# Two-sequence pre-norm transformer layer on 8 cores: the quantized GELU chain regrouped into three VectorE phases with one wait per step

## Chip, cores, metric

One Trainium2 chip, 8 cores. Every core runs the same program on two of the 16 sequences; the cores do not talk to each other. The metric is the device time of one execution in microseconds, that of the slowest core. Engines: TensorE (PE in the rows; PEld are its weight loads), VectorE (DVE), ScalarE (ACT), GpSimd (POOL) and SyncE (SP), the last two issuing DMAs here.

## The reference

```python
# x: (16, 2048, 1024) fp32
x = x + attn(layernorm(x))          # 16 heads of 64, w_qkv 1024x3072, w_proj 1024x1024
h = float2fix(layernorm(x) @ w1 + b1)      # w1 1024x4096; round to multiples of 1/256
xq = float2fix(h)
y = interp(xq, 33 points of exact GELU on [-4, 4]); y = where(xq > 4, xq, where(xq < -4, 0, y))
h = float2fix(float2fix(y))
x = x + float2fix(h @ w2 + b2)             # w2 4096x1024
```

`float2fix` rounds to multiples of 2^-8. The GELU is piecewise linear between the 33 points, so the kernel quantizes, finds the segment and the fraction, takes GELU at both ends of the segment, and interpolates.

## The kernel before

The program is a list of events in the order of emission, one list per engine; each engine runs its own in order, and counting semaphores join them: `c_pe` for PE, `c_v` for DVE, `c_s` for ACT. A wait is always on a count.

Stage A (0 to some 2200 us) is the first layer norm, QKV, attention and the output projection. The change does not touch it. Its layer norm shows (L204, L206, L216) an operation of DVE followed by a drain and a no-op that carries the increment, and ACT waiting for it.

Stage B is the feed-forward part: 8 blocks (`bi`) of 512 tokens, in each 32 column groups of 128 (`hm`), together 256 steps `g` or `h`. The main loop runs over `g`. In step `g` it emits, in this order:

- the w2 matmuls of the block before, `w2_mm` (L1073, 32 matmuls, 8 such groups to a block, at `hm` 3, 6, ..., 24), and their output eviction `w2_ev` on DVE (L1097, L1102, L1104, at `hm` 5, 8, ..., 26);
- the DMAs of w1 on GpSimd (L798);
- `act_E012(g)`: 8 W1 matmuls into one of two halves of `pA` (L935), free again when the eviction of `g-2` is done; the eviction on ACT (L950, times 256 plus bias, into `ft`); on DVE clamp and round (L961, drain, L964);
- pieces of the layer norm for the next block, in `hm` 3 to 20: loads; statistics on DVE (L841 to L846) and the square root on ACT (L855, with a table load ahead of it and one behind it, for the next GELU); reciprocal on DVE (L866, L868) and the apply on ACT (L880); transposes on PE (L894) and the copy of them on DVE (L905);
- `act_E34(g-1)`: ACT scales into `fu5` (L977); DVE rounds, subtracts, adds 0.5 (L985, L987, L990, with drains between);
- `act_E56(g-2)`: ACT computes two GELUs (L1006, L1008); DVE takes the difference and combines (L1017, L1019, L1022, with drains between);
- `act_E78(g-3)`: ACT adds a large constant and rescales into `gbuf` (L1039, drain, L1041).

Before L950, L977, L1006 and L1039 ACT has a `drain` as well, behind the wait. Every DVE group waits for the ACT instruction that feeds it and for nothing later, except that L961 also waits for the GELUs of `h-3`. The w2 matmuls of a block wait until its last `gbuf` is written (`g_done_of`); that happens in step `hm` 2 of the next block. All buffers are rings: `ft` and `fki` of four, `fu5` of three, `fji`, `fgl` of two.

Of the kernel before, what the change touches and what calls it, by code (L numbers as in the profile page):

```python
# [10 lines left out]
ALU = mybir.AluOpType  # L11
# [38 lines left out]
def build():  # L50
# [15 lines left out]
    p = Prog()  # L66
    with es:
# [844 lines left out]

        e1_hist = {}
        e5_hist = {}
        e6_hist = {}
        e8_hist = {}

        def act_E012(h):
            bi, hm = divmod(h, 32)
            hb = hm % 2  # L920
            i = h % 3
            i4 = h % 4
            grp = hm // 2
            sl = grp % 2

            def ev(t, bi=bi, hm=hm, hb=hb, sl=sl,
                   xd=xn2_ready[bi], wl=(w1load[(bi, grp)] if hm % 2 == 0 else None),
                   ag=e1_hist.get(h - 2)):
                t.wait_ge(c_v.sem, xd)
                if wl is not None:  # L930
                    t.wait_ge(c_lw[sl].sem, wl)
                if ag is not None:
                    t.wait_ge(c_s.sem, ag)
                for dc in range(NDC):
                    ins = t.matmul(pA[:, hb * 512:(hb + 1) * 512],  # L935
                                   w1s[:, sl, dc, (hm % 2) * 128:(hm % 2 + 1) * 128],
                                   xn2[:, bi % 2, dc, :],
                                   start=(dc == 0), stop=(dc == NDC - 1))
                ins.then_inc(c_pe.sem, 1)
            p.on("tensor", ev)  # L940
            c_pe.n += 1
            w1mm[(bi, grp)] = c_pe.n
            w1_pe = c_pe.n

            def ev(sc, hm=hm, hb=hb, i4=i4, w=w1_pe, vg=e6_hist.get(h - 4)):
                sc.wait_ge(c_pe.sem, w)
                if vg is not None:
                    sc.wait_ge(c_v.sem, vg)
                sc.drain()
                sc.activation(ft[:, i4, :], pA[:, hb * 512:(hb + 1) * 512], AF.Identity,  # L950
                              bias=b256[:, hm:hm + 1], scale=256.0).then_inc(c_s.sem, 1)
            p.on("scalar", ev)
            c_s.n += 1
            e1_hist[h] = c_s.n
            sid_done = c_s.n

            def ev(v, i=i, i4=i4, w=sid_done, sg=e5_hist.get(h - 3)):
                v.wait_ge(c_s.sem, w)
                if sg is not None:
                    v.wait_ge(c_s.sem, sg)  # L960
                v.tensor_scalar(fki[:, i4, :], ft[:, i4, :], -1152.5, 1152.5,  # L961
                                ALU.max, ALU.min)
                v.drain()  # L963
                v.tensor_scalar(ft[:, i4, :], fki[:, i4, :], MC, -MC,  # L964
                                ALU.add, ALU.add).then_inc(c_v.sem, 1)
            p.on("vector", ev)
            c_v.n += 1
            e1_hist[(h, "va")] = c_v.n

        def act_E34(h):  # L970
            i = h % 3
            i4 = h % 4

            def ev(sc, i=i, i4=i4, w=e1_hist[(h, "va")]):
                sc.wait_ge(c_v.sem, w)
                sc.drain()  # L976
                sc.activation(fu5[:, i, :], ft[:, i4, :], AF.Identity,  # L977
                              bias=p155[:, 0:1], scale=1.0 / 64.0).then_inc(c_s.sem, 1)
            p.on("scalar", ev)
            c_s.n += 1  # L980
            u5_done = c_s.n

            def ev(v, i=i, i4=i4, w=u5_done):
                v.wait_ge(c_s.sem, w)
                v.tensor_scalar(fki[:, i4, :], fu5[:, i, :], MC, -MC, ALU.add, ALU.add)  # L985
                v.drain()  # L986
                v.scalar_tensor_tensor(ft[:, i4, :], fki[:, i4, :], -1.0, fu5[:, i, :],  # L987
                                       ALU.mult, ALU.add)
                v.drain()
                v.tensor_scalar(fu5[:, i, :], ft[:, i4, :], 0.5, None,  # L990
                                ALU.add).then_inc(c_v.sem, 1)
            p.on("vector", ev)
            c_v.n += 1
            e1_hist[(h, "vb")] = c_v.n

        def act_E56(h):
            i = h % 3
            i4 = h % 4
            j = h % 2

            def ev(sc, i=i, j=j, w=e1_hist[(h, "vb")], fg=e6_hist.get(h - 2)):
                sc.wait_ge(c_v.sem, w)
                if fg is not None:
                    sc.wait_ge(c_v.sem, fg)
                sc.drain()
                sc.activation(fgl[:, j, :], fki[:, i4, :], AF.Gelu, bias=neg4[:, 0:1],  # L1006
                              scale=0.25)
                sc.activation(fji[:, j, :], fki[:, i4, :], AF.Gelu, bias=neg375[:, 0:1],  # L1008
                              scale=0.25).then_inc(c_s.sem, 1)
            p.on("scalar", ev)  # L1010
            c_s.n += 1
            e5_hist[h] = c_s.n
            s3_done = c_s.n

            def ev(v, i=i, i4=i4, j=j, w=s3_done):
                v.wait_ge(c_s.sem, w)
                v.tensor_sub(ft[:, i4, :], fji[:, j, :], fgl[:, j, :])  # L1017
                v.drain()  # L1018
                v.scalar_tensor_tensor(fki[:, i4, :], ft[:, i4, :], 256.0, fu5[:, i, :],  # L1019
                                       ALU.mult, ALU.mult)  # L1020
                v.drain()
                v.scalar_tensor_tensor(fu5[:, i, :], fgl[:, j, :], 256.0, fki[:, i4, :],  # L1022
                                       ALU.mult, ALU.add).then_inc(c_v.sem, 1)
            p.on("vector", ev)
            c_v.n += 1
            e6_hist[h] = c_v.n

        def act_E78(h):
            bi, hm = divmod(h, 32)
            i = h % 3  # L1030
            j = h % 2

            def ev(sc, bi=bi, hm=hm, i=i, j=j, w=e6_hist[h],
                   gg=w2_last_of.get(bi - 2)):
                sc.wait_ge(c_v.sem, w)
                if gg is not None:
                    sc.wait_ge(c_pe.sem, gg)
                sc.drain()  # L1038
                sc.add(fji[:, j, :], fu5[:, i, :], cmc[:, 0:1])  # L1039
                sc.drain()  # L1040
                sc.activation(gbuf[:, bi % 2, hm, :], fji[:, j, :], AF.Identity,  # L1041
                              bias=nmc256[:, 0:1],
                              scale=1.0 / 256.0).then_inc(c_s.sem, 1)
            p.on("scalar", ev)
            c_s.n += 1
            e8_hist[h] = c_s.n

        w2_pe_of = {}

# [77 lines left out]
            ln2_C1(0, tt)  # L1127
            xn2_ready[0] = ln2_C2(0, tt)

        w2mm_marks = (3, 6, 9, 12, 15, 18, 21, 24)  # L1130
        w2ev_marks = (5, 8, 11, 14, 17, 20, 23, 26)
        NG = NB * NHM
        for g in range(NG + 3):
            if g < NG:
                bi, hm = divmod(g, NHM)
                if bi > 0 and hm in w2mm_marks:
                    w2_mm(bi - 1, w2mm_marks.index(hm))
                if bi > 0 and hm in w2ev_marks:
                    w2_ev(bi - 1, w2ev_marks.index(hm))
                if hm % 2 == 0 and 2 <= hm // 2 + 1 <= 15:  # L1140
                    w1_group_load(bi, hm // 2 + 1)
                if hm == 30 and bi + 1 < NB:
                    w1_group_load(bi + 1, 0)
                act_E012(g)
                if hm == 31 and bi + 1 < NB:
                    w1_group_load(bi + 1, 1)
                if bi + 1 < NB and 3 <= hm <= 20:
                    tt, st = divmod(hm - 3, 4)
                    if st == 0 and hm >= 3 and tt < 4:
                        ln2_L(bi + 1, tt)  # L1150
                    elif st == 2:
                        ln2_A(bi + 1, tt)
                    elif st == 3:
                        ln2_B(bi + 1, tt)
                    elif st == 1 and tt >= 1:
                        ln2_C1(bi + 1, tt - 1)
                        xn2_ready[bi + 1] = ln2_C2(bi + 1, tt - 1)
            if g >= 1 and g - 1 < NG:
                act_E34(g - 1)
            if g >= 2 and g - 2 < NG:  # L1160
                act_E56(g - 2)
            if g >= 3 and g - 3 < NG:
                act_E78(g - 3)
                if (g - 3) % NHM == NHM - 1:
                    g_done_of[(g - 3) // NHM] = c_s.n
        for j in range(8):
            w2_mm(NB - 1, j)
            w2_ev(NB - 1, j)
# [55 lines left out]
```

## Time and profile before

| | us |
|---|---|
| median of 2 runs | 3985.48 |
| lowest, highest | 3984.56, 3986.4 |
| profiled execution, its time | 3982.74 |
| its span on the slowest core (core 2) | 3980.4 |
| spans of the 8 cores | 3956.7 to 3980.4 |
| busy: PE / DVE / ACT / POOL | 2656.2 / 2078.0 / 2432.4 / 674.0 |

The busy times are sums over two stages of different kind. In stage B, from the first eviction at 2303.4 us to the last at 3902.5 us, ACT and DVE work on the GELU chain, 6 and 8 operations of 128x512 to a step, while PE multiplies. After it PE does the last block's w2 matmuls alone. In the rows a number in brackets at the end is the idle time of that engine before the operation, with the operation that ended it.

### The profile page before, as it was taken

Reading aid. Unit: us, or ns where it says so; the run is one execution under the profiler, and the core shown is the slowest. Engines: PE = TensorE matmul, PEld = TensorE weight load, DVE = VectorE, ACT = ScalarE, POOL = GpSimd, SP = SyncE. Lnnn points to the kernel's source line nnn. Section 1 sums busy time; section 2 is a strip of 40 time slices with the busy share of each in tenths; the row PEclk is TensorE's granted clock in tenths of the full one; section 3 lists DMA queues with packets and bytes.
Section 4 is the critical chain, followed back from the end, with each engine's and each line's share of the span. In section 5 each row is a group of like instructions: output and inputs, shape, how many; then the busy total and the mean of one; then the engine's idle time right before and its main releaser. Section 6 shows DMA issues by size and latency. Waiting matters only on the chain.

```text
span 3980.4 us, 42173 instructions; the slowest of 8 cores (3956.7 to 3980.4 us)
## 1 busy us (share of the span) xinstructions
PE 2656.2 (67%) x10880; PEld 935.7 (24%) x10880; DVE 2078.0 (52%) x3166; ACT 2432.4 (61%) x2861; POOL 674.0 (17%) x1234
## 2 busy tenths in 40 slices
PE   0494757667678976777777245766667666767676
PEld 0241212211113421121111111222222222222232
DVE  2203433434340234343434268687778777777894
ACT  1232848676672185766758068676767677777782
POOL 1010000000001000000000233233333333333340
PEclk9997989998988998888889567877888787878898
DMA  5122110010103100000010654343434444443451
GB/s 108 51 36 90 30 54 31 25 34 4 44 5 82 25 3 25 24 14 34 5 44 4 136 76 63 57 84 63 81 57 74 75 71 64 78 67 71 68 82 49
DMA packets 204583, 207.58 MB, mean 52 GB/s; under 512 B 23744, under 2 KB 167104, under 8 KB 204352
## 3 DMA queue, kind: packets, MB, share of 16 engines
q0 software_dynamic: 169792, 95.82, 19.1%
q1 hardware_dynamic: 34560, 109.07, 8.2%
q8 instruction: 98, 1.61, 0.2%
q14 instruction: 133, 1.09, 0.1%
HBM read 257.52 MB, written 33.55 MB: 73 GB/s over the span
## 4 chain that ended last, share of the span: by engine, by line
PE 29%; ACT 18%; DVE 15%; DVEq 14%; issue 8%; ACTq 7%; DMA 7%; POOL 1%; SPq 0%; POOLq 0%
ACT PTb L625 12%; PE pAT L639 6%; PE pA L329 6%; PE pA L612 5%; DMA xstream<-x 5%; PE pBT L641 4%; DVEq L1018 3%; DVEq L963 3%; DVE ft L987 3%; PE pA L1073 3%; DVE fki L1019 3%; PE pA L363 3%; ACTq L976 3%; DVEq L986 2%; ACTq L1038 2%
## 5 line engine op out<-in xcount | busy, mean ns | idle before, releaser
L625 ACT ACTIVATE PTb<-pA,negB 128x1024 bf16<-128x1024 f32 x1024 | 1105.9, 1113 | 467.4 <-PE pA L615 447.0
L935 PE MATMUL pA<-xn,w1s 128*128 128x512 bf16 x2048 | 632.9, 470 | 474.8 <-ACT ft L950 454.4
L798 POOL DMA_DIRECT2D w1s<-w x1024 | 563.1, 579 | 1067.5 <-PE pA L935 1042.1
L639 PE MATMUL pAT<-PTb,vtm 128*65 128x512 bf16 x1024 | 409.6, 400 | 270.1 <-ACT PTb L625 202.7
L1073 PE MATMUL pA<-w2b,gbuf 128*128 128x512 bf16 x2048 | 479.1, 395 | 94.0 <-ACT gbuf L1041 94.0
L612 PE MATMUL pA<-qfm,kfm 64*128 64x512 bf16 x1024 | 405.9, 407 | 53.4 <-DVEq L713 52.2
L935 PEld LDWEIGHTS pA<-xn,w1s 128*128 128x128 bf16 x2048 | 220.3, 113 | 854.7 <-issue 717.2
L641 PE MATMUL pBT<-PTb,vtm 128*65 128x512 bf16 x1024 | 409.7, 400 | 0.0
L615 PE MATMUL pA<-qfm,kfm 64*128 64x512 bf16 x1024 | 406.2, 407 | 0.0
L582 POOL DMA_DIRECT2D attn<-stgB x64 | 33.6, 525 | 1730.9 <-PE pBT L641 1268.0
L1073 PEld LDWEIGHTS pA<-w2b,gbuf 128*128 128x128 bf16 x2048 | 208.1, 102 | 362.7 <-issue 147.1
L498 DVE COPY uAB<-pAT 65x512 f32<-65x512 f32 x64 | 43.9, 686 | 415.1 <-PE pBT L641 410.4
L950 ACT ACTIVATE ft<-pA,b 128x512 f32<-128x512 f32 x256 | 176.0, 688 | 121.9 <-PE pA L935 101.6
L639 PEld LDWEIGHTS pAT<-PTb,vtm 128*65 128x65 bf16 x1024 | 112.5, 110 | 579.2 <-issue 579.2
L329 PE MATMUL pA<-xnfm,wstr 128*128 128x512 bf16 x1024 | 225.5, 384 | 9.2 <-DVEq L713 8.1
L510 DVE RECIPROCAL rbsb<-uAB 1x512 bf16<-1x512 f32 x64 | 214.0, 3344 | 11.7 <-issue 9.0
L1039 ACT ACTIVATE fji<-fu,cmc 128x512 f32<-128x512 f32 x256 | 184.8, 722 | 44.9 <-DVE fu L1022 24.8
L518 DVE RECIPROCAL rbsb<-uAB 1x512 bf16<-1x512 f32 x64 | 210.2, 3285 | 0.0
L1006 ACT ACTIVATE fgl<-fki,neg 128x512 f32<-128x512 f32 x256 | 184.8, 722 | 35.2 <-DVE fu L990 17.5
L612 PEld LDWEIGHTS pA<-qfm,kfm 64*128 64x128 bf16 x1024 | 91.1, 93 | 480.3 <-issue 479.0
L977 ACT ACTIVATE fu<-ft,p 128x512 f32<-128x512 f32 x256 | 184.8, 722 | 27.3 <-DVE ft L964 6.6
L376 DVE TENSOR_TENSOR vtm<-pA,bvbc 128x512 bf16<-128x512 f32 x64 | 44.4, 694 | 293.8 <-PE pA L363 293.8
(90 smaller groups left out, 3178.4 us busy)
## 6 DMA issues: line engine op xcount, KB each, us to landing
w1s<-w POOLq DMA_DIRECT2D x1024, 64.0 KB, 2.5
xstream<-x SPq DMA_DIRECT2D x80, 512.0 KB, 3.8
x1rd<-x1s SPq DMA_DIRECT2D x64, 512.0 KB, 4.5
x1s<-x1t SPq DMA_DIRECT2D x32, 512.0 KB, 2.9
out<-outt SPq DMA_DIRECT2D x64, 256.0 KB, 2.3
wstr<-wqkv POOLq DMA_DIRECT2D x96, 128.0 KB, 5.2
w2b<-w POOLq DMA_DIRECT2D x32, 256.0 KB, 25.6
attn<-stgB POOLq DMA_DIRECT2D x64, 64.0 KB, 1.9
```

The source lines that it names most:

```text
L329: ins = t.matmul(psl[bi], wstr[:, g_ % 2, dc, mq * 128:(mq + 1) * 128], xnfm[:, dc, tb * 512:(tb + 1) * 512], start=(dc == 0), stop=(dc == ...
L510: v.reciprocal(rbsb[64:65, 0:512], uAB[64:65, 0, :]).then_inc(c_v.sem, 1)
L518: v.reciprocal(rbsb[64:65, 512:1024], uAB[64:65, 1, :]).then_inc(c_v.sem, 1)
L612: t.matmul(pA[:, off:off + 512], kfm[0:64, pr, ko:ko + 128], qfm[0:64, pr, qs:qs + 512], start=True, stop=True, skip_group_check=True)
L615: t.matmul(pA[:, off + 512:off + 1024], kfm[64:128, pr, ko:ko + 128], qfm[64:128, pr, qs:qs + 512], start=True, stop=True, skip_group_chec ...
L625: sc.activation(PT[:, kt % 2, :], pA[:, off:off + 1024], AF.Exp, bias=negB[:, 0:1], scale=SCALE).then_inc(c_s.sem, 1)
L639: t.matmul(pAT[0:65, :], lhs[:, 2 * pr, :], PT[:, kt % 2, 0:512], start=(kt == 0), stop=(kt == NKT - 1), skip_group_check=True)
L641: t.matmul(pBT[0:65, :], lhs[:, 2 * pr + 1, :], PT[:, kt % 2, 512:1024], start=(kt == 0), stop=(kt == NKT - 1), skip_group_check=True).the ...
L798: gp.dma_start(out=w1s[:, sl, dc, :], in_=w1[dc * 128:(dc + 1) * 128, grp * 256:(grp + 1) * 256]).then_inc(c_lw[sl].sem, 16)
L935: ins = t.matmul(pA[:, hb * 512:(hb + 1) * 512], w1s[:, sl, dc, (hm % 2) * 128:(hm % 2 + 1) * 128], xn2[:, bi % 2, dc, :], start=(dc == 0) ...
L977: sc.activation(fu5[:, i, :], ft[:, i4, :], AF.Identity, bias=p155[:, 0:1], scale=1.0 / 64.0).then_inc(c_s.sem, 1)
L1073: ins = t.matmul(pA[:, 1024 + ob * 512:1024 + (ob + 1) * 512], gbuf[:, bi % 2, hm, tt * 128:(tt + 1) * 128], w2b[:, hm, nb * 512:(nb + 1) ...
```

## The change

The chain is regrouped. ACT's parts become `act_S1` (L950's eviction), `act_S2` (L977), `act_S3` (the two GELUs) and `act_S4`, emitted in the same places and the same order. Their drains behind the wait are gone, but for the one before the GELUs and the one inside `act_S4`. The eight DVE operations of a step leave their functions and are emitted at the end of step `k` by `act_V(k)`, in three groups: P, Q and R. Each group holds one operation of `k`, `k-1` and `k-2` (R only of the last two) and ends in one drain that carries the increment; the drains inside the groups are gone. `act_V(k)` waits once, for the highest ACT count among S1 of `k`, S2 of `k-1` and S3 of `k-2`. ACT's waits follow: S1(h) for Q of `h-2`, S2(h) for Q of `h`, S3(h) for P of `h+1`, S4(h) for R of `h+2`. The w2 matmuls and evictions are emitted one step later.

```diff
-            def ev(sc, hm=hm, hb=hb, i4=i4, w=w1_pe, vg=e6_hist.get(h - 4)):
+            def ev(sc, hm=hm, hb=hb, i4=i4, w=w1_pe, vg=incQ.get(h - 2)):
                 sc.wait_ge(c_pe.sem, w)
                 if vg is not None:
                     sc.wait_ge(c_v.sem, vg)
-                sc.drain()
                 sc.activation(ft[:, i4, :], pA[:, hb * 512:(hb + 1) * 512], AF.Identity,
                               bias=b256[:, hm:hm + 1], scale=256.0).then_inc(c_s.sem, 1)
...
-            def ev(sc, i=i, i4=i4, w=e1_hist[(h, "va")]):
+            def ev(sc, i=i, i4=i4, w=incQ[h]):
                 sc.wait_ge(c_v.sem, w)
-                sc.drain()
                 sc.activation(fu5[:, i, :], ft[:, i4, :], AF.Identity,
                               bias=p155[:, 0:1], scale=1.0 / 64.0).then_inc(c_s.sem, 1)
...
-            def ev(sc, i=i, j=j, w=e1_hist[(h, "vb")], fg=e6_hist.get(h - 2)):
+            def ev(sc, i4=i4, j=j, w=incP[h + 1]):
                 sc.wait_ge(c_v.sem, w)
                 sc.drain()
                 sc.activation(fgl[:, j, :], fki[:, i4, :], AF.Gelu, bias=neg4[:, 0:1],
                               scale=0.25)
...
+        def act_V(k, NG):
+            def ev(v, k=k, NG=NG, w=e5_hist.get(k - 2), w2=u5_hist.get(k - 1),
+                   w3=e1_hist.get(k)):
+                ww = max(x for x in (w, w2, w3, 0) if x is not None)
+                if ww > 0:
+                    v.wait_ge(c_s.sem, ww)
+                if k < NG:
+                    v.tensor_scalar(fki[:, k % 4, :], ft[:, k % 4, :], -1152.5, 1152.5,
+                                    ALU.max, ALU.min)
+                if 0 <= k - 1 < NG:
+                    v.tensor_scalar(fki[:, (k - 1) % 4, :], fu5[:, (k - 1) % 3, :],
+                                    MC, -MC, ALU.add, ALU.add)
+                if 0 <= k - 2 < NG:
+                    v.tensor_sub(ft[:, (k - 2) % 4, :], fji[:, (k - 2) % 2, :],
+                                 fgl[:, (k - 2) % 2, :])
+                v.drain().then_inc(c_v.sem, 1)
+            p.on("vector", ev)
+            c_v.n += 1
+            incP[k] = c_v.n
+
+            def ev(v, k=k, NG=NG):
+                if k < NG:
+                    v.tensor_scalar(ft[:, k % 4, :], fki[:, k % 4, :], MC, -MC,
+                                    ALU.add, ALU.add)
+                if 0 <= k - 1 < NG:
+                    v.scalar_tensor_tensor(ft[:, (k - 1) % 4, :], fki[:, (k - 1) % 4, :],
+                                           -1.0, fu5[:, (k - 1) % 3, :],
+                                           ALU.mult, ALU.add)
+                if 0 <= k - 2 < NG:
+                    v.scalar_tensor_tensor(fki[:, (k - 2) % 4, :], ft[:, (k - 2) % 4, :],
+                                           256.0, fu5[:, (k - 2) % 3, :],
+                                           ALU.mult, ALU.mult)
+                v.drain().then_inc(c_v.sem, 1)
+            p.on("vector", ev)
+            c_v.n += 1
+            incQ[k] = c_v.n
+
+            def ev(v, k=k, NG=NG):
+                if 0 <= k - 1 < NG:
+                    v.tensor_scalar(fu5[:, (k - 1) % 3, :], ft[:, (k - 1) % 4, :],
+                                    0.5, None, ALU.add)
+                if 0 <= k - 2 < NG:
+                    v.scalar_tensor_tensor(fu5[:, (k - 2) % 3, :],
+                                           fgl[:, (k - 2) % 2, :], 256.0,
+                                           fki[:, (k - 2) % 4, :],
+                                           ALU.mult, ALU.add)
+                v.drain().then_inc(c_v.sem, 1)
+            p.on("vector", ev)
+            c_v.n += 1
+            incR[k] = c_v.n
...
-        w2mm_marks = (3, 6, 9, 12, 15, 18, 21, 24)
-        w2ev_marks = (5, 8, 11, 14, 17, 20, 23, 26)
+        w2mm_marks = (4, 7, 10, 13, 16, 19, 22, 25)
+        w2ev_marks = (6, 9, 12, 15, 18, 21, 24, 27)
...
+            if 0 <= g - 1 < NG:
+                act_S2(g - 1)
+            if 0 <= g - 2 < NG:
+                act_S3(g - 2)
+            if 0 <= g - 3 < NG:
+                act_S4(g - 3)
...
+            if g <= NG + 1:
+                act_V(g, NG)
```

## Rows read from the trace of the kernel before

**Rows 1.** Timeline, ACT: start us, us, engine, line; first eviction of blocks 0, 1, 7; last.
```profile
2303.41 0.69 ACT L950 ACTIVATE ft<-pA,b 128x512 f32<-128x512 f32 x1 [20.91 <-PE pA L935]
...
2483.92 0.69 ACT L950 ACTIVATE ft<-pA,b 128x512 f32<-128x512 f32 x1
...
3735.03 0.69 ACT L950 ACTIVATE ft<-pA,b 128x512 f32<-128x512 f32 x1
...
3902.50 0.69 ACT L950 ACTIVATE ft<-pA,b 128x512 f32<-128x512 f32 x1
```

**Rows 2.** Stretches: from:to, length, busy PE, PEld, DVE, ACT, POOL; clock, DMA, GB/s.
```profile
2900.00:3100.00 200.00, 135.31 (x533) 55.00 (x532) 153.51 (x295) 143.07 (x199) 65.98 (x120) 0.81 0.43 72
```

**Rows 3.** Timeline, ACT, one plain step of block 3.
```profile
2903.44 0.72 ACT L977 ACTIVATE fu<-ft,p 128x512 f32<-128x512 f32 x1
2904.24 0.72 ACT L1006 ACTIVATE fgl<-fki,neg 128x512 f32<-128x512 f32 x1
2904.87 0.71 ACT L1008 ACTIVATE fji<-fki,neg 128x512 f32<-128x512 f32 x1
...
2907.25 0.69 ACT L950 ACTIVATE ft<-pA,b 128x512 f32<-128x512 f32 x1
2908.03 0.72 ACT L977 ACTIVATE fu<-ft,p 128x512 f32<-128x512 f32 x1
```

**Rows 4.** Timeline, DVE, one step and an output eviction.
```profile
3079.57 0.43 DVE L964 TENSOR_SCALAR ft<-fki 128x512 f32<-128x512 f32 x1
3079.91 0.42 DVE L985 TENSOR_SCALAR fki<-fu 128x512 f32<-128x512 f32 x1
3080.41 0.69 DVE L987 SCALAR_TENSOR_TENSOR ft<-fki,fu 128x512 f32<-128x512 f32 x1
...
3083.04 0.69 DVE L1022 SCALAR_TENSOR_TENSOR fu<-fgl,fki 128x512 f32<-128x512 f32 x1
3083.65 0.68 DVE L1097 SCALAR_TENSOR_TENSOR w2scr<-pA,b2bc 128x512 f32<-128x512 f32 x1
...
3085.53 0.42 DVE L961 TENSOR_SCALAR fki<-ft 128x512 f32<-128x512 f32 x1
```

**Rows 5.** Timeline, PE and ACT: start of block 3; W1 matmuls behind idle time.
```profile
2916.59 8.57 PE L1073 MATMUL pA<-w2b,gbuf 128*128 128x512 bf16 x32 [11.20 <-ACT gbuf L1041]
...
2927.08 0.69 ACT L950 ACTIVATE ft<-pA,b 128x512 f32<-128x512 f32 x1 [10.74 <-PE pA L935]
...
2949.32 3.57 PE L935 MATMUL pA<-xn,w1s 128*128 128x512 bf16 x8 [8.63 <-ACT ft L950]
```

**Rows 6.** Timeline, stage A: DVE with drain and no-op, and ACT waiting for it.
```profile
61.13 0.15 DVE L204 TENSOR_SCALAR ln2d<-ln2d 128x1 f32<-128x1 f32 x1
61.46 0.69 DVE L268 COPY xnfm<-pT 128x1024 bf16<-128x1024 bf16 x1 [0.17 <-issue]
61.47 0.20 ACT L216 ACTIVATE ln2d<-ln2d 128x1 f32<-128x1 f32 x1 [6.11 <-DVEq L206]
```

**Rows 7.** Timeline, DVE and ACT, a statistics step of block 3.
```profile
2969.70 0.67 DVE L841 BATCH_NORM_STATS2 ln2d<-x1rd 128x6 f32<-128x512 f32 x1
...
2971.33 0.15 DVE L846 TENSOR_SCALAR ln2d<-ln2d 128x1 f32<-128x1 f32 x1
...
2975.90 0.71 ACT L1008 ACTIVATE fji<-fki,neg 128x512 f32<-128x512 f32 x1
...
2976.71 0.69 DVE L1017 TENSOR_TENSOR ft<-fji,fgl 128x512 f32<-128x512 f32 x1 [1.00 <-ACT fji L1008]
```

**Rows 8.** Timeline, DVE and ACT, the apply step behind it.
```profile
2979.99 0.16 DVE L866 RECIPROCAL ln2d<-ln2d 128x1 f32<-128x1 f32 x1
2980.22 0.21 DVE L868 TENSOR_SCALAR ln2d<-ln2d 128x1 f32<-128x1 f32 x1
...
2983.38 0.71 ACT L1008 ACTIVATE fji<-fki,neg 128x512 f32<-128x512 f32 x1
```

**Rows 9.** Timeline, DVE, the copy of the transposed layer norm.
```profile
2964.25 0.67 DVE L905 COPY xn<-pT 128x1024 bf16<-128x1024 bf16 x1
```

More of the change, by code:

```diff
@@ L914, in build, with act_S1 @@
         e5_hist = {}
-        e6_hist = {}
         e8_hist = {}
-        def act_E012(h):
+        incP = {}
+        incQ = {}
+        incR = {}
+        u5_hist = {}
+        def act_S1(h):
             bi, hm = divmod(h, 32)
             hb = hm % 2
-            i = h % 3
             i4 = h % 4
@@ L954, in act_E012, with act_S2 @@
             e1_hist[h] = c_s.n
[L955 to L970, printed above, removed]
+        def act_S2(h):
             i = h % 3
             i4 = h % 4
-            def ev(sc, i=i, i4=i4, w=e1_hist[(h, "va")]):
+            def ev(sc, i=i, i4=i4, w=incQ[h]):
                 sc.wait_ge(c_v.sem, w)
-                sc.drain()
                 sc.activation(fu5[:, i, :], ft[:, i4, :], AF.Identity,
@@ L980, in act_E34, with act_S3 @@
             c_s.n += 1
[L981 to L997, printed above, removed]
+            u5_hist[h] = c_s.n
+        def act_S3(h):
             i4 = h % 4
             j = h % 2
-            def ev(sc, i=i, j=j, w=e1_hist[(h, "vb")], fg=e6_hist.get(h - 2)):
+            def ev(sc, i4=i4, j=j, w=incP[h + 1]):
                 sc.wait_ge(c_v.sem, w)
-                if fg is not None:
-                    sc.wait_ge(c_v.sem, fg)
                 sc.drain()
@@ L1012, in act_E56, with act_S4 @@
             e5_hist[h] = c_s.n
[L1013 to L1028, printed above, removed]
+        def act_S4(h):
             bi, hm = divmod(h, 32)
@@ L1031, in act_E78, with ev @@
             j = h % 2
-            def ev(sc, bi=bi, hm=hm, i=i, j=j, w=e6_hist[h],
+            def ev(sc, bi=bi, hm=hm, i=i, j=j, w=incR[h + 2],
                    gg=w2_last_of.get(bi - 2)):
@@ L1037, in ev @@
                     sc.wait_ge(c_pe.sem, gg)
-                sc.drain()
                 sc.add(fji[:, j, :], fu5[:, i, :], cmc[:, 0:1])
@@ L1128, in build @@
             xn2_ready[0] = ln2_C2(0, tt)
-        w2mm_marks = (3, 6, 9, 12, 15, 18, 21, 24)
-        w2ev_marks = (5, 8, 11, 14, 17, 20, 23, 26)
+        w2mm_marks = (4, 7, 10, 13, 16, 19, 22, 25)
+        w2ev_marks = (6, 9, 12, 15, 18, 21, 24, 27)
         NG = NB * NHM
-        for g in range(NG + 3):
+        for g in range(NG + 6):
             if g < NG:
@@ L1143, in build @@
                     w1_group_load(bi + 1, 0)
-                act_E012(g)
+                act_S1(g)
                 if hm == 31 and bi + 1 < NB:
@@ L1148, in build @@
                     tt, st = divmod(hm - 3, 4)
-                    if st == 0 and hm >= 3 and tt < 4:
+                    if st == 0 and tt < 4:
                         ln2_L(bi + 1, tt)
@@ L1157, in build @@
                         xn2_ready[bi + 1] = ln2_C2(bi + 1, tt - 1)
[L1158 to L1163, printed above, removed]
+            if 0 <= g - 1 < NG:
[4 more added lines that the diff above has]
+                act_S4(g - 3)
                 if (g - 3) % NHM == NHM - 1:
                     g_done_of[(g - 3) // NHM] = c_s.n
+            if g <= NG + 1:
+                act_V(g, NG)
         for j in range(8):
```

## The prediction

> **What bounds the kernel now.** I read the table of stretches first, then the timelines of ACT and DVE in one block of the feed-forward stage, then what stands at its edges. The change touches only that stage, 256 steps in 8 blocks of 32, one S1 eviction (L950) to a step. Block 0 lasts from 2303.41 to 2483.92, 180.5 us; blocks 1 to 6 end at 3735.03, 1251.1 / 6 = 208.5 us each; block 7 has its last eviction 167.5 us later [rows 1]. In 200 us of the middle DVE is busy 153.5, ACT 143.1, PE 135.3 [rows 2]: nobody is full on average, because the block is a mixture.
>
> A plain step takes 4.59 us on ACT (L977 to L977) and ACT does not stop in it [rows 3]: a start-to-start distance is 0.63 where no drain stands between two operations (L1006 to L1008), 0.80 where one does, so an ACT drain costs 0.17. DVE is as full: L964 to L985 is 0.34 without a drain, L985 to L987 0.50 with one, an operation of 0.69 takes 0.61 without (L1022 to L1097) and 0.69 + 0.08 = 0.77 with [rows 4]. Four short and four long ones with five drains: 4 x 0.34 + 4 x 0.61 + 5 x 0.16 = 4.60. So ACT and DVE are both the bound of a plain step, each drifting up to a step against the other. On top come, per middle block: four layer-norm statistics steps (ACT waits for DVE, then two table loads), four layer-norm apply steps, eight output evictions of 1.88 us of DVE (L1097 to the next L961) [rows 4], and one start of block in which ACT waits 10.74 us for PE, which runs 32 w2 matmuls (8.57 us) ahead of the W1 matmuls that the eviction needs [rows 5].
>
> **What goes.** Three of five ACT drains of a step (before L950, L977, L1039): 3 x 0.17 = 0.51, ACT's own work falls to 4.1 us. Two of DVE's five: the new group has P = 0.34 + 0.34 + 0.77 = 1.45, Q = 0.34 + 0.61 + 0.77 = 1.72, R = 0.34 + 0.77 = 1.11, together 4.28. If engines alone counted, a step would now cost 4.28.
>
> **What comes: a closed loop.** Follow the new waits. DVE's group V(g) waits once, for the highest ScalarE count: the two gelus S3(g-2), third in ACT's step g. In ACT's queue S2(g-1) stands ahead of S3(g-2), and it waits for Q of V(g-1). So V(g) cannot start before: P and Q of V(g-1), S2, S3. Before, V started piecewise on older results; now no drift is allowed. Its length: P + Q = 3.17 to the next start, less the 0.08 of the gap, plus DVE to ACT 0.19 (end of L204 61.28 to L216 61.47, with a drain and an increment between, as in the new group) [rows 6] = 3.28; S2 to S3 0.80 (this drain stays), 0.63, 0.71 for the second gelu [rows 3]; ACT to DVE 0.10 (L1008 ends 2976.61, L1017 starts 2976.71) [rows 7]. Sum 5.52 us, for a plain step that took 4.59. DVE then idles 1.24 of it. ACT's S4 and S1 lie under P and Q: from the second gelu to a possible S2 it took 3.16 (2904.87 to 2908.03) [rows 3], now 3.16 - 0.51 = 2.65, while Q's release comes 0.71 + 0.10 + 3.28 = 4.09 after it: ACT idles 1.44.
>
> Unknown: whether a drain that carries the increment costs more than the plain 0.08. Above: L204 ends at 61.28 and the next DVE operation starts at 61.46, 0.18 with drain and no-op [rows 6], 0.10 more, of which P's alone is new to my loop: 5.62. Below: 0.10 in place of 0.19 for DVE to ACT, as from ACT to DVE: 5.43. I take 5.52, nearer to the row of the same kind.
>
> The DVE price rests on 0.34 and 0.61 where no drain stands. The Trainium skill (VectorE: DVE Perf Modes, The DRAIN you can't avoid) says that a flush follows each VectorE operation, that it can't be skipped by chaining without semaphores, and that one should save operations, not semaphores. The row L964 to L985 [rows 4] disagrees with the first part; what the rule would give stands among the rivals.
>
> **Steps with more in them.** All DVE extras now stand between V(g-1) and V(g).
> - Output eviction: 4.28 + 1.88 = 6.16, since the loop (5.52) is shorter. It waits for w2 matmuls issued two steps earlier, long done. Moving each mark by one step changes nothing here.
> - Statistics step: ACT's square root waits for all of V(g-1), 4.28, and the statistics, 1.78 (2969.70 to 2971.48); from there to the start behind the gelu 5.23 (to 2976.71) [rows 7], less the drain before L977, 0.17: 11.1. With an eviction 13.0.
> - Apply step: 4.28 + 0.44 (2979.99 to 2980.43) + 3.66 (to the end of L1008, 2984.09) + 0.10 - 0.17 [rows 8] = 8.3, with an eviction 10.2.
> - The copy L905, 0.67 at most [rows 9], hides in DVE's 1.24 of idle time, but not in hm 12, which has an eviction: 6.8.
> - Start of block: with the mark at 4, PE runs the W1 matmuls of hm 3 first, so ACT's S1(3) passes, and S1(4) is what waits. It comes one step later and has ACT's idle time behind it: 10.7 - 5.5 - 1.4 = 3.8 instead of 10.7, so 9.3 for this step. If that cover were gone, it would cost 10.7 as before.
> - Elsewhere PE has cover: behind a w2 group stand at worst 3.57 (the W1 matmuls at a low clock) [rows 5] before it and after it, 3.57 + 8.57 + 3.57 = 15.7, against three steps of 16.6. GpSimd's w1 loads wait for PE and have longer steps now. The last groups of the run keep their length within some 3 us (two partial groups V more): 2 us, an estimate.
>
> **The sum.** Block 0 (no w2): 24 x 5.52 + 4 x 11.1 + 4 x 8.3 = 210.1; its first two steps have no gelu yet (2 x 1.34) and shorter groups: 206, against 180.5: +26. A middle block, evictions at hm 6, 9, 12, 15, 18, 21, 24, 27, of which 9 is a statistics step, 6 and 18 apply steps: 18 plain x 5.52 = 99.4; 4 x 6.16 = 24.6; 6.8; 3 x 11.1 + 13.0 = 46.3; 2 x 8.3 + 2 x 10.2 = 37.0; 9.3; together 223.4 against 208.5: +14.9, six times +89. Block 7 to its last eviction: 22 x 5.52 + 8 x 6.16 + 9.3 = 180.0 against 167.5: +12.5. End +2. Sum +129.5 us. The profiled execution took 3982.7 us, 2.8 below the median of 3985.5; it becomes 4112, the median 4115 us, 3.3% slower. Inside it, 7 x 6.9 = 48 us are gained at block starts, and 154 x 0.93 = 143 us are lost in the plain steps; the rest is the balance of the longer and shorter steps with more in them.
>
> **The rivals.**
> - A. The loop does not close and DVE's 4.28 is the step. That is the other side: 0.3 less in each of 256 steps and 4.3 less at seven block starts (the wait of 10.7 comes one step of 4.3 later): 77 + 30 = 107 us, 3878, 2.7% faster. The full queues of ACT and DVE speak for it, the order of the waits against it. It decides if a plain step comes out below 4.6. It would need V(g) to be free of the gelus of the same step, and the code reads otherwise. 6%.
> - B. The loop closes but is short, 5.2 or less, because waits overlap with the drains: 154 x 0.33 = 51 us less and some more in the steps with layer norm: 4050, within 2%. No row gives a latency under 0.10, of which the loop has two. 10%.
> - C. The rule quoted above holds in the new groups: each DVE operation costs 0.50 or 0.77. P + Q grow by 0.64, the group to 5.08: 154 x 0.64 + 100 x 0.8 = 179 us more: 4294. The row of 0.34 is against it. 3%.
> - D. PE, fed at a slower pace, is granted the low one of its two clocks (1.2 against 2.4 GHz) and its w2 group takes twice 7 to 8.6 us: some 8 us more at seven block starts and in some of the other 49 groups 1 to 2 us: +56 to +120: 4171 to 4235. For it: the middle has a mean granted clock of 0.81 and W1 matmuls behind idle time take 3.57 [rows 2, 5]. Against: a w2 group behind 11.2 us of idle time took 8.57, so the clock came back within it [rows 5]. 10%.
>
> **How the numbers follow.** The forecast has 71%. Its own range: the loop at 5.43 to 5.62 gives -14 to +15, a missing or doubled cover at the block starts -27 to +48, the latencies in the layer-norm and eviction steps +-20: 4075 to 4175. To hold 8 in 10 it takes in what lies between it and B below, and half of D above: 4060 to 4185. A and B lie below, C and the other half of D above. Two per cent (about what a measurement of this kernel tells from no change) is 4065: faster 0.06 (A), same 0.12 (B and the lowest 2% of the forecast), slower 0.82.
>
> **What would show it.** In the new profile a plain step of 5.5 us from L950's successor to itself, ACT idle 1.4 us before S2, waiting for the drain of Q, and DVE idle 1.2 us before P, waiting for the second gelu; eviction steps of 6.2; statistics steps of 11.1; at block starts a wait of ACT for PE of about 5 us instead of 10.7. Busy times of ACT and DVE all but unchanged, the stage longer. A plain step at 4.3 with DVE never idle would prove me wrong (A), one of 6.2 with DVE operations 0.50 apart likewise (C); a w2 group of 14 us would be D.

## The result, and the profile after

The changed kernel takes 4143.8 us (median of 11 runs) against 3986.0 us (10 runs), a ratio of 1.038 with a 95% interval of 1.035 to 1.042: 3.8% slower. Forecast were 4115 us and 3.3%, in a range of 4060 to 4185. The profiled execution took 4138.8 us. (Ratios, and times said to be of one or two runs, leave out the runs in which the cores of a die had a lower granted clock; before_late has no row in the table below because its profiled execution was such a run.) The span is 4137.2 us against 3980.4, 156.8 us more. 155.9 of them lie between the first and the last S1 eviction: 2302.75 to 4057.74 us, where it was 2303.41 to 3902.50 [rows 1]. S1's eviction is L951 now, S2 L963, the gelus L976 and L978, S4 L994 and L996; P is L1010, L1013, L1016; Q is L1025, L1028, L1032; R is L1042, L1045.

The page and the table of stretches, of the changed kernel (columns of the second as in [rows 2]):

```profile
PE 2696.9 (65%) x10747; PEld 942.9 (23%) x10880; DVE 2022.9 (49%) x3166; ACT 2367.6 (57%) x2861; POOL 666.5 (16%) x1234
```

```profile
2900.00:3100.00 200.00, 126.52 (x473) 49.76 (x480) 136.43 (x274) 123.63 (x181) 61.34 (x112) 0.79 0.41 68
```

DVE and ACT are busy 55 and 65 us less in sum than before. That is not less work: the records of neighbours with no drain between them overlap by 0.09 us (0.43 long, 0.34 apart), and busy time counts the overlap once, 2 x 0.09 x 256 = 46 us on DVE and 3 x 0.09 x 256 = 69 us on ACT. In 200 us of the stage both are busy less as well: 136.4 and 123.6 against 153.5 and 143.1 [rows 2]. Their operations did not become slower, the engines stand still. Where, the waits of the stage say (engine, line, what it waited for: us in total, times, longest):

```profile
DVE fki L1010 <- ACT fji L978: 449.1, 214, 6.5
ACT fu L963 <- DVEq L1035: 296.2, 190, 2.9
ACT L855 <- DVE ln2d L846: 148.9, 28, 6.5
ACT xn2tm L880 <- DVE ln2d L868: 112.7, 27, 5.6
```

The first two are the two halves of the loop: P waits for the second gelu, S2 waits for Q's drain. One plain step in the timeline of both engines:

```profile
3205.59 0.43 DVE L1010 TENSOR_SCALAR fki<-ft 128x512 f32<-128x512 f32 x1 [1.22 <-ACT fji L978]
...
3207.07 0.43 DVE L1025 TENSOR_SCALAR ft<-fki 128x512 f32<-128x512 f32 x1
...
3208.01 0.68 DVE L1032 SCALAR_TENSOR_TENSOR fki<-ft,fu 128x512 f32<-128x512 f32 x1
3208.82 0.43 DVE L1042 TENSOR_SCALAR fu<-ft 128x512 f32<-128x512 f32 x1
3208.82 0.72 ACT L963 ACTIVATE fu<-ft,p 128x512 f32<-128x512 f32 x1 [1.36 <-DVEq L1035]
3209.16 0.69 DVE L1045 SCALAR_TENSOR_TENSOR fu<-fgl,fki 128x512 f32<-128x512 f32 x1
3209.62 0.72 ACT L976 ACTIVATE fgl<-fki,neg 128x512 f32<-128x512 f32 x1
3210.25 0.71 ACT L978 ACTIVATE fji<-fki,neg 128x512 f32<-128x512 f32 x1
...
3211.06 0.43 DVE L1010 TENSOR_SCALAR fki<-ft 128x512 f32<-128x512 f32 x1 [1.22 <-ACT fji L978]
```

From P to P it is 5.47 us, and no piece is free: P 1.48, Q 1.75, S2 starts with the release of Q, 0.80 to the first gelu, 0.63 to the second, 0.71 for it, 0.10 to the next P.

A step with an output eviction, DVE's timeline, and ACT's at the start of block 4 follow.

```profile
3374.44 0.69 DVE L1045 SCALAR_TENSOR_TENSOR fu<-fgl,fki 128x512 f32<-128x512 f32 x1
3375.45 0.69 DVE L1103 SCALAR_TENSOR_TENSOR w2scr<-pA,b2bc 128x512 f32<-128x512 f32 x1 [0.33 <-issue]
...
3377.34 0.42 DVE L1010 TENSOR_SCALAR fki<-ft 128x512 f32<-128x512 f32 x1
```

```profile
3206.79 0.67 ACT L951 ACTIVATE ft<-pA,b 128x512 f32<-128x512 f32 x1
...
3218.49 0.69 ACT L951 ACTIVATE ft<-pA,b 128x512 f32<-128x512 f32 x1 [6.13 <-PE pA L937]
...
3222.51 0.67 ACT L951 ACTIVATE ft<-pA,b 128x512 f32<-128x512 f32 x1
```

The eviction itself takes 1.89 (3375.45 to 3377.34), but L1103 starts 1.01 behind the start of R's last operation, not 0.77: 0.33 us of idle time, with no engine to wait for, stand behind the end of that operation. At the start of the block S1(4) now waits 6.13 us for PE where S1(3) waited 10.74 [rows 5], and the next eviction follows after 4.02.

### The profile page after: what moved, and what is told of

Its sections match the earlier page's. It is cut to its first block, busy times and chain, and to the rows that moved or that the text cites. A ratio compares the mean times of both kernels' runs of the same rounds, so it can differ in the third digit from the quotient of the medians.

```text
span 4137.2 us, 39751 instructions; the slowest of 8 cores (4125.2 to 4137.2 us)
## 1 busy us (share of the span) xinstructions
PE 2696.9 (65%) x10747; PEld 942.9 (23%) x10880; DVE 2022.9 (49%) x3166; ACT 2367.6 (57%) x2861; POOL 666.5 (16%) x1234
## 4 chain that ended last, share of the span: by engine, by line
PE 29%; DVE 18%; ACT 15%; DVEq 12%; ACTq 11%; issue 8%; DMA 6%; POOL 1%; SPq 0%; POOLq 0%
ACT PTb L625 11%; PE pAT L639 6%; DVEq L1035 5%; ACTq L995 5%; PE pA L329 5%; PE pA L612 5%; DMA xstream<-x 5%; ACTq L975 4%; PE pBT L641 4%; DVE ft L1016 3%; PE pA L1079 3%; PE pA L363 3%; DVEq L1018 3%; DVE ft L1025 2%; DVE fki L1010 2%
## 5 line engine op out<-in xcount | busy, mean ns | idle before, releaser
L937 PE MATMUL pA<-xn,w1s 128*128 128x512 bf16 x2000 | 662.9, 490 | 558.7 <-ACT ft L951 531.0
L963 ACT ACTIVATE fu<-ft,p 128x512 f32<-128x512 f32 x256 | 183.9, 718 | 299.0 <-DVEq L1035 299.0
L1010 DVE TENSOR_SCALAR fki<-ft 128x512 f32<-128x512 f32 x256 | 109.7, 428 | 472.9 <-ACT fji L978 450.4
L951 ACT ACTIVATE ft<-pA,b 128x512 f32<-128x512 f32 x256 | 171.1, 669 | 65.0 <-PE pA L937 65.0
L976 ACT ACTIVATE fgl<-fki,neg 128x512 f32<-128x512 f32 x256 | 184.7, 722 | 20.6 <-DVEq L1049 1.8
L996 ACT ACTIVATE gbuf<-fji,nmc 128x512 bf16<-128x512 f32 x256 | 184.8, 722 | 17.9 <-issue 0.4
```

Source lines behind the costliest of these rows:

```text
L937: ins = t.matmul(pA[:, hb * 512:(hb + 1) * 512], w1s[:, sl, dc, (hm % 2) * 128:(hm % 2 + 1) * 128], xn2[:, bi % 2, dc, :], start=(dc == 0) ...
```

## The experiments

The theory is the closed loop of the prediction; its rivals are the amount of work on DVE or ACT, the drains, and the moved places of the w2 groups. Since runs differ ahead of the stage, most by up to 12 us, before_marks by 30 and marks_back by 84, the table gives for each kernel the time between its first and its last S1 eviction, in the profiled execution, beside the length of a plain step (start to start of that eviction) in it.

| kernel | first to last S1 | against | expected | plain step |
|---|---|---|---|---|
| before | 1599.1 | | | 4.59 |
| changed | 1755.0 | +155.9 (before) | +127.5 | 5.48 |
| twice_in_q | 1843.2 | +88 (changed) | +87 | 5.81 |
| twice_in_r | 1787.1 | +32 (changed) | +32 | 5.48 |
| three_waits | 1626.1 | -129 (changed) | -143 | 4.80 |
| swap | 1619.9 | -135 (changed) | -144 | 4.45 |
| marks_back | 1794.6 | +40 (changed) | +38 | 5.48 |
| before_marks | 1573.5 | -26 (before) | -32 | 4.59 |
| before_nodrain | 1582.2 | -17 (before) | -10 | 4.00 or 4.58 |
| after_late | 1543.0 | -212 (changed) | -180 | 5.48 |
| swap_late | 1398.6 | -356 (changed) | -329 | 4.45 |
| swap_late_split | 1363.1 | -35 (swap_late) | -35 | 4.45 |

**A cost on the loop and off it.** The same short operation, once in Q and once in R; both also lengthen the group V.

```diff
                     v.tensor_scalar(ft[:, k % 4, :], fki[:, k % 4, :], MC, -MC,
                                     ALU.add, ALU.add)
+                    v.tensor_scalar(w2scr[:, 0, :], fki[:, k % 4, :], MC, -MC, ALU.add, ALU.add)
```

```diff
                     v.tensor_scalar(fu5[:, (k - 1) % 3, :], ft[:, (k - 1) % 4, :],
                                     0.5, None, ALU.add)
+                    v.tensor_scalar(w2scr[:, 0, :], ft[:, (k - 1) % 4, :], 0.5, None, ALU.add)
```

> The changed kernel with one VectorE operation more per step, a rounding of fki of step k into a scratch tile, put into group Q, between the start of V(g) and the release of S2 (the result is not used). Loop theory: Q lies on the loop, so a plain step grows by the 0.34 us that a short operation takes without a drain, 5.48 to 5.82, and every other step too, because the group V is 0.34 longer: 256 x 0.34 = 87 us, 4144 to about 4231. Rival, the step is bound by ACT's work or by something outside the chain: plain steps stay at 5.48, under 4180.

> The changed kernel with the same sort of operation (a short one into a scratch tile, result not used) put into group R, behind the release of S2. Loop theory: R is not on the loop, VectorE idles 1.22 us behind it, so a plain step stays at 5.48; only the steps that have an output eviction or a layer-norm piece between the groups (94 of 256) grow by 0.34: +32 us, about 4176. Rival, VectorE's amount of work sets the step: the same +87 us as with the operation in Q, 4231.

Measured: 4235.8 us (ratio 1.058) with the operation in Q, 4180.5 (1.047) with it in R. In Q a plain step grows from 5.48 to 5.81, in R it stays at 5.48. The timeline of twice_in_r shows the operation (L1044) and S2 started before it, released by the same drain as ever:

```profile
3274.72 0.43 DVE L1042 TENSOR_SCALAR fu<-ft 128x512 f32<-128x512 f32 x1
3274.72 0.72 ACT L963 ACTIVATE fu<-ft,p 128x512 f32<-128x512 f32 x1 [1.36 <-DVEq L1035]
3275.07 0.42 DVE L1044 TENSOR_SCALAR w2scr<-ft 128x512 f32<-128x512 f32 x1
```

So in the changed kernel the amount of DVE's work does not set the plain step; where it stands does.

**Two operations taken off the loop.** One wait for all of P becomes one per operation.

```diff
-                ww = max(x for x in (w, w2, w3, 0) if x is not None)
-                if ww > 0:
-                    v.wait_ge(c_s.sem, ww)
                 if k < NG:
+                    v.wait_ge(c_s.sem, w3)
                     v.tensor_scalar(fki[:, k % 4, :], ft[:, k % 4, :], -1152.5, 1152.5,
                                     ALU.max, ALU.min)
                 if 0 <= k - 1 < NG:
+                    v.wait_ge(c_s.sem, w2)
                     v.tensor_scalar(fki[:, (k - 1) % 4, :], fu5[:, (k - 1) % 3, :],
                                     MC, -MC, ALU.add, ALU.add)
                 if 0 <= k - 2 < NG:
+                    v.wait_ge(c_s.sem, w)
...
```

> The changed kernel with the one wait of act_V split in three: the clamp of k waits for S1(k), the rounding of k-1 for S2(k-1), and only the subtraction of k-2 for the gelus S3(k-2). Nothing else. Loop theory: the two short operations (0.34 each) leave the loop, a plain step goes from 5.48 to 4.80; statistics and apply steps lose 0.68 as well, the eviction steps (6.47, bound by VectorE) stay: 154 x 0.68 + 56 x 0.68 = 143 us, about 4001. Rival, the drains that carry the increments or the removed overlap of PE cause the loss: no change, 4144.

Measured: 4018.6 us, ratio 1.0073 (1.0022 to 1.0124), plain step 4.80 to 4.81. The whole drop of 0.68 came from where DVE waits; every drain is still there. The missing 14 us are spread. In block 0 the four statistics steps gain 0.29 each, not 0.68 (11.29 to 11.00), and the block 18.9 of 21.8; a middle block gains 16.2 of 17.7, with 0.6 of the gap in the statistics steps and 0.2 at its start, where S1(4) waits for PE whatever the loop does (10.8 to 11.6, then 4.0); block 7 gains 13.0 of 15.0. Why a statistics step gains less was not looked into.

**The loop opened.** Two calls in the main loop change places, so that ACT runs the gelus ahead of S2.

```diff
-            if 0 <= g - 1 < NG:
-                act_S2(g - 1)
             if 0 <= g - 2 < NG:
                 act_S3(g - 2)
+            if 0 <= g - 1 < NG:
+                act_S2(g - 1)
```

> The changed kernel with one exchange in ACT's order: the gelus S3(g-2), which need only P of V(g-1), are emitted ahead of S2(g-1), which needs Q. Loop theory: from the start of V(g-1) to Q's release 3.23, S2 0.72, latency 0.10 = 4.05 us, less than the group V itself (1.48 + 1.75 + 0.34 + 0.88 = 4.45), so the loop no longer sets the step: plain steps 5.48 to 4.45, 154 x 1.03 = 159 us less; at the seven block starts 1.0 + 1.4 less cover, +15; about 4000. Rival, V still waits for S2 and S2 for Q, so the exchange brings nothing or only the 1.34 of the gelus in part: plain steps 5.0 or more, 4070 to 4144.

Measured: plain steps 4.45, to the hundredth what DVE's group takes with one wait behind R's drain. The waits of the stage are turned round: S2's is down from 296 to 14.2 us, P's sum went from 449 to 293 us in 67 places, nearly all of them layer-norm steps and block starts.

```profile
DVE fki L1010 <- ACT fu L963: 292.8, 67, 7.7
ACT L855 <- DVE ln2d L846: 161.0, 28, 7.3
ACT xn2tm L880 <- DVE ln2d L868: 116.0, 28, 5.6
ACT fji L994 <- DVEq L1049: 76.7, 190, 1.0
```

The ratio is 1.0077 (1.0003 to 1.0152): with the loop gone the regrouped kernel is still no faster than the one before, though its plain step is 0.14 shorter. The reason stands in the second and third line: both of ACT's layer-norm parts wait until a whole group V is done (the apply 116.0 us in sum, before 54.9). It is cleanest in block 0, which has no w2 work: its four statistics and four apply steps take 80.4 us, before 74.3 (in block 3 it is 89.2 against 82.0, with evictions in other steps). In the mean middle block, 212.1 us against 208.5, the three steps at the start (hm 2 to 4) are 5.2 us shorter and the steps hm 5 to 20 8.4 longer, 127.5 against 119.1. In block 0 those are 5.9 longer (116.9 against 111.0); the other 2.5 are that the five evictions among them add 10.6 us here and 8.1 before.

**Other parts of the change, one by one.** marks_back undoes only the places of the w2 groups; before_marks is the kernel before with only these moved:

```diff
-        w2mm_marks = (3, 6, 9, 12, 15, 18, 21, 24)
-        w2ev_marks = (5, 8, 11, 14, 17, 20, 23, 26)
+        w2mm_marks = (4, 7, 10, 13, 16, 19, 22, 25)
+        w2ev_marks = (6, 9, 12, 15, 18, 21, 24, 27)
```

> The changed kernel with the old places of the w2 matmuls (hm 3, 6, ...) and evictions (hm 5, 8, ...). Theory: at the seven block starts S1(3) instead of S1(4) waits for the w2 group, with one step of 5.5 less cover; the two steps at the start now cost 4.7 more than two plain ones, they would cost about 10.2 more: +38 us, about 4182. Rival, the moved marks are part of the loss: faster than 4144.

> The kernel before with only the places of the w2 matmuls and evictions moved one step later, as in the change. Theory: seven times a step of 4.59 covers part of the 10.7 that ACT waits: 7 x 4.6 = 32 us less, 3954. Rival, the moved marks bring nothing or a later eviction collides with the layer-norm statistics: 3986 or more.

before_marks has a ratio of 0.990 (0.985 to 0.996), 3950.6 us at best; a middle block falls from 208.5 to 204.8. marks_back took 4258.8 us, but its profiled execution was 84 us later than the changed kernel before the first step of the stage, where the code is the same, and the ratio 1.059 has an interval of 1.045 to 1.074. The granted clock goes with that delay: 0.82 from 500 to 1500 us, where the changed kernel had 0.89 and 0.91. Within the stage it is +40 where +38 was expected, and in its other three runs the cores of the die with a clock of 0.83 to 0.84 end by 4181, 4176 and 4192 us, where a die of the changed kernel at that clock ends by 4134 to 4142. The moved marks are a gain, in both directions.

before_nodrain takes the three ACT drains out of the kernel before, at the three places shown in the change.

```diff
                 sc.wait_ge(c_v.sem, w)
-                sc.drain()
                 sc.activation(fu5[:, i, :], ft[:, i4, :], AF.Identity,
```

> The kernel before with only the three ACT drains removed that the change removes (before L950, L977, L1039). Theory: VectorE is full in a plain step too (4.60 us), so plain steps stay at 4.59 and only the 56 layer-norm steps lose 0.17 each: 10 us, about 3977. Rival, ACT alone was the bound: plain steps fall toward 4.1, 150 x 0.5 = 75 us less, 3910.

One run, 3967.3 us, against 3983.6 us of the fastest run of the kernel before on that chip; one run gives no interval, and the reading rests on the steps. Behind each layer-norm step its plain steps are 4.00 us, ACT's own pace; there DVE has no backlog that counts yet. But the statistics steps grow in return (in the middle blocks from 12.7 to 13.3 us on average), since the square root's waits for L846 grow from 142.3 to 175.7 us in sum, and from hm 22 on the steps without an eviction are about 4.6 again. The statement "VectorE is full in a plain step too" holds as a mean, not in each step.

**The layer-norm steps.** ACT's square root and apply are emitted one step later, behind S1, while DVE's statistics and reciprocal stay where they are: `ln2_A` and `ln2_B` keep DVE's part, `ln2_A2` is the square root, `ln2_B2` the apply.

```diff
-                    if st == 0 and tt < 4:
+                    if st == 0 and tt >= 1:
+                        ln2_B2(bi + 1, tt - 1)
+                    if st == 0 and tt < 4:
                         ln2_L(bi + 1, tt)
                     elif st == 2:
                         ln2_A(bi + 1, tt)
                     elif st == 3:
+                        ln2_A2(bi + 1, tt)
                         ln2_B(bi + 1, tt)
```

> The changed kernel with only ACT's two layer-norm parts emitted one step later (no exchange of S2 and S3). Theory: plain steps stay at 5.48, since the loop is untouched; the three steps statistics, apply, plain (11.3 + 8.5 + 5.5) become 6.2 + 7.1 + 5.5, 6.4 us less, 28 times: about -180, 3964. So the late parts and the opened loop add up to what both gave together (3780 against 4144). Rival, the late parts are worth their gain only where the loop is open: over 4050.

> The kernel before with only ACT's two layer-norm parts emitted one step later. Theory: the gain of the late parts has nothing to do with the change: statistics, apply, plain (12.7 + 7.5 + 4.6) become 6.4 + 7.0 + 5.9, 5.5 us less, 28 times: -154, about 3832; the regrouped kernel with the exchange (3780) is then faster by only some 50 us, of which 30 are the moved marks. Rival, VectorE's ungrouped waits stop it behind the late square root: 3900 or more.

> The exchange of swap, and ACT's two layer-norm parts (square root, apply) emitted one step later than VectorE's statistics and reciprocal, behind S1, so that ACT need not stand still until a whole group V and the statistics are done. Theory: statistics step 11.3 to about 6.4, the step with the table loads 7.2, the apply step 5.4; a middle block about 184 us against 227.8 of the changed kernel and 208.5 of the kernel before; about 3815 us, 4% faster than before. Rival, PE (7.07 + 3 x 1.89 = 12.7 us of work per three steps at the high clock, 17.8 with W1 matmuls at the low one) or GpSimd's w1 loads become the bound below 13.4 us per three steps: 3900 or more.

On the changed kernel: 3931.0 us, ratio 0.985 (0.983 to 0.988). On the kernel before: 3827.5 us, ratio 0.960 (0.957 to 0.963). With the exchange as well: 3780.1 us, ratio 0.946 (0.940 to 0.952). In the stage, the late parts alone give 212 us, the exchange alone 135, both 356: they add up, to within 9 us. The late parts give 32 us more than expected: in a middle block the evictions of hm 6 and 18, 2.1 us each in the changed kernel, now cost nothing (the steps with them take 7.6 and 7.5, those without 7.5), 6 x 4.2 = 25 us. In swap_late the square root's table load waits 1.86 us, and P is not held:

```profile
3053.28 0.15 DVE L846 TENSOR_SCALAR ln2d<-ln2d 128x1 f32<-128x1 f32 x1
3053.39 0.43 DVE L1016 TENSOR_SCALAR fki<-ft 128x512 f32<-128x512 f32 x1
3053.55 1.28 ACT L858 ACT_TABLE_LOAD   x1 [1.86 <-DVE ln2d L846]
```

Before, from the end of L846 to a DVE operation that needed the gelus it was 5.23 us [rows 7]; here P starts 0.11 behind L846's start.

**A step further.** The groups of 32 w2 matmuls in two halves, in two steps.

```diff
-                for hm in range(NHM):
+                for hm in range(NHM // 2):
...
+                if bi > 0 and hm - 1 in w2mm_marks:
+                    w2_mm2(bi - 1, w2mm_marks.index(hm - 1))
```

> The kernel swap_late with each group of 32 w2 matmuls emitted in two halves of 16 in two following steps, so that the W1 matmuls of a step wait behind 16 and not 32. Theory: the two steps at a block start, 15.9 us now against 8.9 plain, fall to about 11 (a half group of 4.3 to 4.7 us plus 1.9 against a step of 4.45), 7 x 4 = 28 us less, and the stalls at hm 12 (9.2 instead of 5) get shorter: about 3745. Rival, PE gets idle time between the halves and its clock falls: no gain, 3780 or more.

Two runs took 3747.1 and 3750.4 us; ratio 0.940 (0.936 to 0.943), the fastest kernel here. A block start costs 7.2 to 8.7, 5.2 and 4.0 in three steps instead of 11.2 to 12.2, 4.0 and 4.6.

## Why the prediction was right, and by how much it missed

- The loop. Forecast 5.52 for a plain step, measured 5.48. The mechanism holds from three sides: work on it counts in full (twice_in_q), work off it counts for nothing in plain steps (twice_in_r), and taking two operations off it (three_waits) or turning S2 and S3 (swap) gives 4.80 and 4.45 as worked out beforehand. Two of its terms were off and cancelled in part: P + Q is 1.48 + 1.75 = 3.23, not 3.17, since a drain that carries an increment costs 0.12 to 0.13 and not 0.08; from the end of Q's last operation to S2 it is 0.13 (3208.69 to 3208.82), not the 0.19 that I took from [rows 6]. The question that I kept open, what such a drain costs, came out between its two ends.
- The steps with more in them. Forecast 6.16 for an eviction step, measured 6.47. This is the term that was mis-sized. Behind a drain with an increment the next group's waits are no longer hidden under a running operation: 0.19 of idle time with one wait (L905, L841), 0.33 with three (L1103), where L1022 to L1097 had none [rows 4]. I had seen the 0.18 in [rows 6] and charged it only to P, where it does not stand, and not behind R, where it does. An eviction step is 0.31 longer than forecast, 0.24 of it from this (1.01 against 0.77 behind R) and 0.06 from P and Q; statistics and apply steps are about 0.2 longer (11.29 against 11.1, 8.47 against 8.3), 0.11 of it from the one wait behind R (0.88 against 0.77) and 0.06 from P and Q.
- The block start. Forecast 9.3 for the step with the stall and 5.5 for the next; measured 15.5 for the two (mean of seven; 14.6 to 16.2), 0.7 more. The cover was worked out rightly, but the w2 group was taken from one block. From the start of the group to the first W1 matmul behind it block 3 took 8.4 us, the shortest of the seven before (8.4 to 9.6, mean 8.8); in the changed kernel it is 8.2 to 9.8, mean 9.1. So half of the 0.7 was there before the change. In both kernels the length goes with the granted clock in it: 0.84 at 8.2 us, 0.82 at 8.4, 0.77 at 8.9, 0.70 at 9.8.
- The sum. Block 0: +24.9, forecast +26. Middle blocks 1366.6 / 6 = 227.8 us against 208.5: +19.3, forecast +14.9; of the 4.4, 8 x 0.31 = 2.5 are the evictions, 8 x 0.2 = 1.6 the layer-norm steps, 0.7 the start, less 18 x 0.02 = 0.4 in the plain ones (5.50 on average), which is 4.4. Block 7: +15.5, forecast +12.5. End: +1.6, forecast +2. Together 28 us too little, 6 x 4.4 of it in the middle blocks; the profiled execution exceeds its forecast of 4112 by 27, since its stage also began 0.7 us earlier. The forecast that the busy times stay was off by the 55 and 65 us above: it did not reckon that busy time counts an overlap once.
- The rivals. A (the loop does not close) is out: 5.48, not 4.3. B (a short loop) is out. C (each operation 0.50 or 0.77) is out: L1010 to L1013 is 0.34 and L1028 to L1032 0.60 in the new groups. The Trainium skill (VectorE: DVE Perf Modes, The DRAIN you can't avoid), from which it comes, says that the flush can't be skipped by chaining operations without semaphores. The same section of the Trainium skill also says that a next operation that is not held starts earlier, and only with that do these rows agree. D (PE at the lower clock) is small: the granted clock in 2900 to 3100 us went from 0.81 to 0.79, and the w2 groups at block starts grew by 0.3 us on average, not by 7 to 8.6.
- Where the gain went that the change does have. DVE's group with two drains fewer is 0.14 us shorter than the step before (swap, 4.45 against 4.59): the two drains are 0.32, and the dearer drains and the wait behind R take back about half. ACT's three drains bring plain steps of 4.00 where DVE is not behind, but 17 us in all (before_nodrain); the moved marks bring 26 us. The loop took back 0.9 in each plain step, and the steps from hm 5 to 20, in which ACT's layer-norm parts wait for a whole group V, take back the rest: that is what swap is left with.

Left open: what sets the granted clock within the w2 group at a block start, and why it was lower in marks_back ahead of the stage.

## What to carry to other kernels

Before merging several waits of a pipelined chain into one, write down for the merged group what it waits for, what that waits for in its own queue order, and whether the path returns to the previous group; if it does, and its sum is longer than each engine's work in a step, that sum is the new step. Here one exchange of two lines in the other engine's order opened it. And try emitting an instruction that waits for a short piece on another engine a step later than that piece, where its result is not needed sooner: that was worth more here (4% on the kernel before) than the regrouping with its loop opened (no gain by itself, and a ratio of 0.946 in place of 0.960 on top).

## What the runs showed of the hardware

- On VectorE, a short 128x512 operation followed by another starts 0.34 us later without a drain, 0.50 with one; a long one 0.60 and 0.77. A drain that carries an increment makes it 0.81, 0.12 behind the end of the last operation. When waits follow such a drain, it is 0.19 us with one wait (L841, L905, and P in swap) and 0.33 with three (L1103), even if all are long satisfied. Without a drain in front a satisfied wait costs nothing: in three_waits the two short operations of P, each with a wait, start 0.34 apart.
- On ScalarE a drain between two operations makes the distance 0.80 us and not 0.63. Taking out the drain before S1's eviction shortened the record of the eviction itself too, from 687 to 668 ns, and the distance to the operation ahead of it from 0.80 to 0.62 us.
